# Eight-stage transformer on one core: the first stage's norm in small steps, a shorter inverse root, and earlier starts for parts of two attentions

## What is computed

```python
x = x + jnp.tanh(g_xattn[0]) * _L0_xattn_ref(32, 64, 256, L0_xattn_w, L0_xattn_u, _layernorm(x, axis=-1), ctx_2048)
x = x + jnp.tanh(g_ffn[0]) * _L0_ffn_ref(_layernorm(x, axis=-1), ...)
x = x + jnp.tanh(g_xattn[1]) * _L1_xattn_ref(_layernorm(x, axis=-1), ctx_2048)
x = x + jnp.tanh(g_ffn[1]) * _L1_ffn_ref(_layernorm(x, axis=-1), ...)
x = x + jnp.tanh(g_xattn[2]) * _L2_xattn_ref(_layernorm(x, axis=-1), ctx_2048, mask_BxSxS2_ff0, ...)
x = x + jnp.tanh(g_ffn[2]) * _L2_ffn_ref(_layernorm(x, axis=-1), ...)
x = x + jnp.tanh(g_xattn[3]) * _L3_xattn_ref(_layernorm(x, axis=-1), ctx_2048, ...)
x = x + jnp.tanh(g_ffn[3]) * _L3_ffn_ref(_layernorm(x, axis=-1), L3_ffn_W1, L3_ffn_W2, L3_ffn_W3)
```

```python
def step(carry, kv_t):
    p, q, o = carry
    kt, vt = kv_t
    no = jnp.maximum(o, u + kt)
    A = jnp.exp(o - no)
    E = jnp.exp(u + kt - no)
    y = (A * p + E * vt) / (A * q + E)
    no2 = jnp.maximum(w + o, kt)
    A2 = jnp.exp(w + o - no2)
    E2 = jnp.exp(kt - no2)
    return ((A2 * p + E2 * vt, A2 * q + E2, no2), y)
```

## Time and profile before

| | us |
|---|---|
| median of 3 runs | 1572.27 (1571.3 to 1572.7) |
| profiled execution | 1573.29 |
| its span, first to last instruction | 1571.5 |
| TensorE busy | 1264.3 (80%) |
| VectorE busy | 973.2 (62%) |
| ScalarE busy | 496.9 (32%) |
| GpSimd busy | 325.8 (21%) |
| granted TensorE clock, mean | 0.916 |

### The profile page before, as it was taken

One profiled execution on the slowest core, in us unless ns is written; L12 is line 12 of the kernel. 1 busy time (PEld: TensorE's weight loads), 2 busy tenths in 40 slices (PEclk: granted clock), 3 DMA queues, 4 the chain that ended last, 5 costly groups with the idle time before them and its releaser, 6 DMA issues.

```text
span 1571.5 us, 19840 instructions
## 1 busy us (share of the span) xinstructions
PE 1264.3 (80%) x6710; PEld 712.7 (45%) x6718; DVE 973.2 (62%) x2359; ACT 496.9 (32%) x684; POOL 325.8 (21%) x334
## 2 busy tenths in 40 slices
PE   0127999999978999967778757656898989999998
PEld 0114444545434456645455423332454445455555
DVE  8994454545255246657778879945888788822222
ACT  3363121222103133322222234522454445541111
POOL 1121000000022500004532434443243324000000
PEclk9986999999989999978978968866999999999999
DMA  9100000002000020011011000013232223100000
GB/s 315 45 14 1 0 0 0 0 0 97 1 20 0 1 68 0 0 27 28 0 27 27 1 23 1 1 29 94 76 93 77 83 74 89 42 1 14 14 14 13
DMA packets 68905, 55.34 MB, mean 35 GB/s; under 512 B 25444, under 2 KB 62180, under 8 KB 68580
## 3 DMA queue, kind: packets, MB, share of 16 engines
q1 hardware_dynamic: 68196, 54.22, 11.5%
q10 hardware_dynamic: 640, 0.26, 0.1%
HBM read 39.45 MB, written 14.68 MB: 34 GB/s over the span
## 4 chain that ended last, share of the span: by engine, by line
PE 63%; DVE 18%; issue 12%; POOL 3%; ACT 2%; DMA 1%; DVEq 0%; SPq 0%; POOLq 0%; ACTq 0%
PE banks L2158 7%; PE banks L1027 7%; PE banks L644 6%; PE banks L427 5%; PE banks L423 5%; PE banks L860 4%; PE banks L1034 4%; PE banks L852 3%; PE banks L434 3%; PE banks L438 3%; PE banks L2123 3%; PE banks L1354 2%; DVE sb_work L2395 1%; PE banks L2108 1%; PE banks L2144 1%
## 5 line engine op out<-in xcount | busy, mean ns | idle before, releaser
L2395 DVE TENSOR_REDUCE sb_work<-banks 128x2 f32<-128x512 f32 x256 | 164.7, 685 | 50.1 <-PE banks L2123 47.8
L2267 ACT ACTIVATE sb_work<-banks 128x1024 f32<-128x1024 f32 x128 | 130.9, 1023 | 129.4 <-PE banks L2144 129.3
L1467 POOL TENSOR_TENSOR sb_work<-sb_work,sb_consts 128x512 f32<-128x512 f32 x64 | 68.6, 1102 | 251.7 <-ACT sb_work L1411 232.6
L544 DVE TENSOR_TENSOR sb_work<-sb_work,banks 128x512 f32<-128x512 f32 x72 | 49.5, 688 | 114.2 <-ACT sb_work L511 114.2
L1027 PE MATMUL banks<-sb_work,sb_shelf 128*128 128x512 f32 x256 | 114.4, 592 | 0.0
L511 ACT ACTIVATE sb_work<-banks 128x512 f32<-128x512 f32 x72 | 42.9, 596 | 169.9 <-PE banks L423 109.4
L644 PE MATMUL banks<-sb_work,sb_ctx_nat 128*64 128x512 f32 (+15 forms) x512 | 90.0, 510 | 7.8 <-DVE sb_work L706 7.8
L1003 POOL TENSOR_TENSOR sb_late<-sb_w2n 128x1024 f32<-128x1024 f32 x10 | 22.7, 2267 | 353.9 <-DVE sb_work L698 353.3
L427 PE MATMUL banks<-sb_work,sb_shelf 128*128 128x512 f32 (+1 forms) x192 | 85.7, 632 | 10.2 <-DVE sb_work L587 8.6
L1106 DVE TENSOR_TENSOR sb_work<-sb_work,banks 128x512 f32<-128x512 f32 x32 | 22.0, 688 | 112.5 <-ACT sb_work L1092 112.5
L423 PE MATMUL banks<-sb_work,sb_shelf 128*128 128x512 f32 (+1 forms) x192 | 78.1, 594 | 0.0
(11 more groups left out here) (296 smaller groups left out, 2511.3 us busy)
## 6 DMA issues: line engine op xcount, KB each, us to landing
sb_work<-scratch SPq DMA_DIRECT2D x64, 192.0 KB
scratch<-sb_work SPq DMA_DIRECT2D x32, 192.0 KB, 2.1
sb_work<-ctx_t SPq DMA_DIRECT2D x16, 256.0 KB, 4.5
scratch<-sb_work SPq DMA_DIRECT2D x32, 128.0 KB, 2.1
sb_work<-ctx_t SPq DMA_DIRECT2D x4, 512.0 KB, 3.6
sb_ctx_nat<-ctx SPq DMA_DIRECT2D x1, 2048.0 KB, 11.1
sb_raw<-wguT SPq DMA_DIRECT2D x1, 2048.0 KB, 15.4
scratch<-sb_work SPq DMA_DIRECT2D x32, 64.0 KB, 1.8
```

The costliest lines, as they stand in the source:

```text
L1467: ins = nc.gpsimd.tensor_tensor(km_[:, hf, k, :, :], keys.unsqueeze(1).broadcast_to([P, 8, SEQ]), hm2.unsqueeze(2).broadcast_to([P, 8, SEQ ...
L2267: nc.scalar.activation(pt3[:, h % 2, :, :], o, ACT.Exp).then_inc(exp3, 1)
L2395: nc.vector.tensor_reduce(out=mx3[:, tc, k, 2 * hp:2 * hp + 2], in_=bank[u % 2].rearrange("p (h s) -> p h s", h=2), axis=AX, op=ALU.max).t ...
```

## The change

It has four parts.

1. **wkv.** `Chain` gets `mark` (count) and `hold` (wait, for all but the last few). The norm of the next block is spread: its four bn_stats now stand at the start of `gaps`, ahead of the scans and for the block after the next; the three merge steps and the eight root steps stand one each between scans, the memset, and the products; the waits between them let one instruction run ahead. `apply_statistics` stands behind the addition that gives den_ready and ahead of the reciprocal. In the rows of after, L340 is the scan of `gaps`, L350 the subtraction, L358 the first product, L363 and L366 the four scans, L371 and L374 the multiplication and the addition that gives den_ready, L380 the reciprocal, L382 the last product, L162 bn_stats, L168-176 and L141-152 the small steps, L195 the apply, L212 the residual.
2. **Inverse root** in 8 linked operations instead of 11, for all stages (the first guess in one operation, one iteration of higher order, one of Newton's).
3. **attn2.** The next block's statistics stand behind `second` of t=1 instead of t=0, and root and apply both at t=2.
4. **attn3's first tiles.** The projections of q and k of tiles 0 and 1 stand in TensorE's queue of bit's last block (into banks 4, 5, 0, 1), their rotates in VectorE's, and three of the four splits at the end of GpSimd's. The buffers for this move from `work` to `raw`.

The core of the diff:

```diff
+        def root(i, v, y, t, y_int):
+            if i == 0:
+                return nc.vector.tensor_scalar(y_int, v.bitcast(I32), -0.5, float(0x5f3759df), ALU.mult, ALU.add)
...
         def rsqrt(link, v, y, t, y_int):
-
-            link(nc.vector.tensor_scalar(y_int, v.bitcast(I32), 1, None, ALU.logical_shift_right))
-            link(nc.vector.tensor_scalar(y_int, y_int, -1.0, float(0x5f3759df), ALU.mult, ALU.add))
-            for _ in range(3):
-                link(nc.vector.scalar_tensor_tensor(out=t, in0=y, scalar=-0.5, in1=y, op0=ALU.mult, op1=ALU.mult))
-                link(nc.vector.tensor_tensor(t, t, v, ALU.mult))
-                link(nc.vector.scalar_tensor_tensor(out=y, in0=t, scalar=1.5, in1=y, op0=ALU.add, op1=ALU.mult))
+            for i in range(ROOT_STEPS):
+                link(root(i, v, y, t, y_int))
...
+        def norm_step(link, i, but=0):
+
+            link.hold(but)
+            if i < 3:
+                link.mark(merge(i))
+            else:
+                link.mark(root(i - 3, ve[:, :], rs[:, :], nt[:, :], rs[:, :].bitcast(I32)))
...
-            def gaps(b):
-
+            def gaps(b, nxt):
+
+                if nxt is not None:
+                    link.mark(tile_statistics(nxt))
                 dve.wait_ge(kT_ready, b + 1)
                 for c in range(KC):
-                    ins = nc.vector.tensor_tensor_scan(o_sh[:, c, 1:BTOK + 1], w_time[:, c, :], kT[:, c, :],
-                                                       0.0, ALU.add, ALU.max)
...
+                    link.mark(nc.vector.tensor_tensor_scan(o_sh[:, c, 1:BTOK + 1], w_time[:, c, :], kT[:, c, :],
+                                                           0.0, ALU.add, ALU.max))
+                    if nxt is not None:
+                        norm_step(link, c, 1)
...
             def block_(b, last):
-                dve.wait_ge(wkv_turned, b + 1)
-                normalise(link, (b + 1) % BLOCKS)
                 dve.wait_ge(wkv_exp, 4 * b + 2)
...
+                    norm_step(link, 5 + 2 * c, 1)
...
                 nc.vector.tensor_tensor(gap, gap, e_old, ALU.add).then_inc(den_ready, 1)
+                norm_step(link, 10)
+                dve.wait_ge(wkv_turned, b + 1)
+                link.hold()
+                apply_statistics((b + 1) % BLOCKS)
                 dve.wait_ge(den_ready, b + 1)
                 link(nc.vector.reciprocal(gap, gap))
...
-                    if t < 3:
-                        normalise(link, (b + 1) % BLOCKS, step=t)
-                    if t == 2 and not last:
-                        query_ints(b + 1)
+                    if t == 1:
+                        normalise(link, (b + 1) % BLOCKS, step=0)
+                    elif t == 2:
+                        normalise(link, (b + 1) % BLOCKS, step=1)
+                        normalise(link, (b + 1) % BLOCKS, step=2)
+                        if not last:
+                            query_ints(b + 1)
...
+                else:
+                    early_project(pe, 0)
                 project(b, 0)
                 if b + 1 < BLOCKS:
                     turn_parts(b + 1)
+                else:
+                    early_project(pe, 1)
                 project(b, 1)
+            early_project(pe, 2)
+            early_project(pe, 3)
             turn_gated(BLOCKS - 1, 2)
...
+            split3(pool, link, 0, 0, 0)
+            split3(pool, link, 1, 0, 1)
+            split3(pool, link, 0, 1, 2)
...
             value(last, 3, 1)
+            early_rotate(dve, 0)
             to_ints(last, 2)
+            early_rotate(dve, 1)
             measure(last, 3)
             to_ints(last, 3)
             finish(last, 1)
+            early_rotate(dve, 2)
             finish(last, 2)
+            early_rotate(dve, 3)
             finish(last, 3)
...
+        EARLY3 = ((4, 0, 0), (5, 0, 1), (0, 1, 0), (1, 1, 1))
...
+            i, m, z = EARLY3[k]
+            for done in (b_silu, bv_ready):
+                pe.wait_ge(done, 8 * (BLOCKS - 1) + 6 + k // 2)
...
             contexts(0)
-            split(0, 0, 0)
-            split(1, 0, 1)
-            split(0, 1, 3)
-            split(1, 1, 4)
+            split(1, 1, 3)
             split(1, 2, 6)
```

## The result

The changed kernel took 1557.18 us, the median of five runs; the kernel before took 1571.3 beside it. The ratio is 0.9908 (95% interval 0.9887 to 0.9929), so it is 14.1 us or 0.9% faster. I had forecast 1569.9, a change of 2.4, with a range from 1558: the time is 0.8 us outside it and the gain is six times the forecast.

A forecast was written before the change was run, and what follows sets the result against it. TensorE bounds 63% of the span and VectorE 18%, with stage 1 VectorE's. Terms 27.3 - 12.35 - 2.4 - 2.1 + 0.3 - 13.15 = -2.4 from 1572.27 give 1569.9 us, range 1558 to 1582.

The forecast's parts named there:

- Stage 1, the wait for ScalarE: Stage 1: VectorE idles about 3.2 us a block waiting for ScalarE's exponentials, costing 0.9 a block.
- Stage 1, the port: Stage 1: the applies wait for GpSimd's three products through a shared port, 5.8 us a block, 23.2 over four blocks.
- no hold: Rival, 7%: in stage 1 the applies run beside GpSimd's products without waiting, -23.2 us, total 1546.7.
- partly held: Rival, 12%: in stage 1 two applies slip in after GpSimd's second product, 8.6 us less, total 1561.3.
- attn2: attn2: the next tile's scores no longer wait behind the norm's statistics, 3.1 us a block; four blocks -12.35.
- slower: Rival, 13%: in attn2 tile 2's scores do not decide, only the root's 0.6 us a block is won; 1579.9.
- Ternary and bit: Ternary and bit: the shorter root on the path wins 2.4 and 2.1 us; the four rotates cost 0.3.
- Start of attn3: Between bit's end and attn3's first scores: the first split and its DRAM write come earlier, -13.15 us.
- The step that failed: MoE, conv, attn3's blocks and had: the shorter root runs beside TensorE work, cost nothing; 0.6 us a block if uncovered.

The follow-up runs named there:

- Experiment 2: The changed kernel with stage 1's four applies moved behind the reciprocal in VectorE's queue; 1534.82 us, ratio 0.9786.
- experiment 6: Kernel before with the new root everywhere but in attn3's norm, 1548.07 us; kernel before with the new root only in attn3's norm, 1565.03 us.
- early_alone: The kernel before with only the early projections, rotates and splits of attn3; 1556.84 us, ratio 0.9925.
- shifted: The kernel before with its first memset written four times, delaying everything behind it by 3.5 us; 1576.18 us, ratio 1.0039.
- s1_of_before, experiment 1: The changed kernel with the first stage's (wkv) VectorE function as before, the other parts kept; 1526.38 us, ratio 0.9725.
- root_alone_padded: The kernel before with the new inverse root alone, plus 84 idle one-column memsets in VectorE's queue before attn3's first reductions; 1551.68 us, ratio 0.9885.

## Why the prediction was wrong, point by point

**Stage 1, the wait for ScalarE: right.** 3.37 us of idle time where 3.2 stood.

**Stage 1, the port: right.** The applies took 6.9 us, the period was 33.9 and not 34.2, the stretch +26.3 and not +27.3. Experiment 2 shows that it is the meeting with GpSimd's products and not the instructions. The order was not quite the forecast's: two applies were through after the first product and one after each of the others, not one, one and two; the sum is the same. The two rivals on this point, no hold and partly held, fell.

**attn2: right in place, small in size.** The wait moved as forecast, and the *slower* rival fell. -14.5 against -12.35. The alone runs show that part of this is clock, which the step did not have (TensorE busy 159.8 us instead of 167.8 with the move alone). The step's own working also does not add up: four blocks at 3.1 are 12.4, and the 0.6 a block for the shorter root, which it names, is not in that; with it the sum would have been -14.8. So the nearness of the number is partly luck.

**Ternary and bit: right.** -2.4 and -2.5 against -2.4 and -1.8.

**Start of attn3: right.** -13.5 against -13.15, and alone -13.3.

**The step that failed** is the last sentence of the prediction's first paragraph: the shorter root "beside TensorE work, and I cost it at nothing there", with 0.6 us a block as the most it could be. It looked for a price along VectorE's path alone. In attn3 the changed kernel is 7.4 us shorter, and 4.9 of that is the third block (81.1 to 76.2), where the shorter program took away the stop of 3.34 us at 1243.42. The windows view over the rest of attn3, before and after:

```profile
1068.94:1394.31 325.37, 293.71 (x2412) 154.26 (x2413) 253.76 (x622) 154.48 (x193) 100.26 (x145) 0.94 0.25 73
```

```profile
1056.86:1374.78 317.92, 292.57 (x2412) 154.12 (x2413) 251.66 (x610) 154.28 (x193) 100.25 (x145) 0.94 0.25 75
```

TensorE is busy for 1.1 us less and idle for 6.3 less. So here it is nearly all waiting time, and the 5 to 7 us of clock that the new root won in the kernels of experiment 6 are hardly seen in the changed one; why, no run shows. The rest is -5.5 in MoE and conv. These stretches do not follow the edit: MoE took 314.8 us in early_alone and shifted, where nothing of it is changed, and 318.1 in s1_of_before and root_alone_padded, which have the new root, so I put them down to scatter of the clock. The two profiles differ by 5 us more than the medians, so that much must be such scatter. Without it the misses of the other lines of the table (7.4 in attn3, 2.15 in attn2, 1.0 in stage 1, 0.7 in bit, 0.35 at the start of attn3) come to 11.6 us, and the medians missed the forecast by 11.7.

**The range.** I widened it by unknown costs of single edits and not by the clock. The four kernels in which the root of attn2 or attn3 was put in or taken out moved by 5 to 13 us, for 2.4 us of VectorE work. The lower end should have been some 10 us lower.

**The sum hid a large loss.** By experiment 1 the change without its first part is 1526.4, 44 us or 2.8% under the kernel before.

## What to carry to other kernels

Where one edit is supposed to win by moving small work under other work, look up what the second engine does at the new place: four 0.4 us instructions of VectorE beside three products of GpSimd cost 5.5 us a block, and nothing when they stand one instruction further back. In a stage in which TensorE waits often, price an edit by the clock as well: the range has to take in the matmuls behind the wait at both levels, as in the two rows of attn2. And search the profile of before for idle time whose releaser is "issue": an edit that changes the length of an engine's program can remove or bring such a stop far away from itself.

## What I had not expected of the hardware

Three linked VectorE operations of 0.2 us less in a block of attn2 went with TensorE's 1116 unchanged instructions being 12.0 us shorter, at a granted clock of 0.88 instead of 0.82. A VectorE program longer by 84 idle memsets had a stop of 7.25 us in the third pass over a code that was unchanged, where the kernel without them had none. And of VectorE's instructions beside GpSimd's products the reciprocal over 128x1024 was not held at all (6.55 us in both places), while three of four tensor_scalars over 128x256 were held for as long as GpSimd's instruction ran (2.16, 2.08 and 2.50 us instead of 0.4).
